# A 39-iteration software pipeline on one core: router products in four column groups, a new order on every engine, and another start

## The chip, the cores and the metric

The kernel runs on one core of a Trainium2 chip. The metric is the device time of one launch in microseconds (us), lower is better. The core has a matrix engine (PE, with its weight loads shown as PEld), a vector engine (DVE), an activation engine (ACT), GpSimd (POOL), and SyncE (SP), which here only issues DMAs. Each engine works through its own list of instructions in order and waits on semaphores for the others.

## The reference

The input x is 8 x 1024 x 256 in float32. Four layers follow one another, each added to a running sum:

```
x = x + gated_linear_attention_and_mlp(layernorm(x))
x = x + mixture_of_experts(layernorm(x))
x = x + tanh_recurrence(layernorm(x))
x = x + mixture_of_experts(layernorm(x))
```

The first layer has its own LayerNorm, a gate `log_sigmoid(h W1 W2 + b) / 16`, a state per head that decays by that gate, a gated output product (`Wo`), and a GELU MLP (`W1`, `W2`). A mixture multiplies every token by all 8 experts (256 x 256), takes router logits (256 to 8), a softmax and the two best experts, and adds the two products with their weights. The recurrence is `h = tanh(x_t B + h A^T)` with 16 states over 1024 steps, then two products.

## The kernel before

**Rounds and stages.** Time is cut into 32 rounds of 32 tokens for all 8 batches, so a round is 256 tokens in two tiles of 128. A round passes through stages, one per iteration; `body(it)` on each engine works on up to eight rounds at once, and `live(it, s)` says whether stage s has one. Iterations 0 to 7 (the fill) are written out, 8 to 31 are a hardware loop, 32 to 38 (the drain) are written out again. The order on each engine is written by hand in its `body`; semaphores count up over the whole launch.

**What stands between what.** The recurrence is the thread on which the rest is strung: `step(k)` on PE (one small product), two tanh on ACT (`state_of(k)`) and one DVE instruction (`split_state(k)`), 32 times a round; each engine has other work between two of them. That work is on PE: `moe` (six products of 512 columns; G1_0 to G1_7 for the first mixture, G2_0 to G2_7 for the second), attention (`scores`, `read_state`, `state_update`, `attend` in 32-wide forms), transposes (T1, T2 of the two mixtures' inputs, Y0, Y1, TR, OG, KT), and the dense products (Z gate, QK, VG, WO, F1, F2).

**The router before.** `logits` takes the transposed tokens `yT` as weights, in two parts (a leading part and its rest), and multiplies by `rws`, the router's two-part weights: for each of 2 tiles and 2 chunks one product of 16 columns and one of 8. The result stands by token, ready for `top_two` on DVE. `yT` comes from T1 by an ACT copy (`lead1`, the leading part) and a DVE subtraction (`rest`, its line is L931).

**Banks.** PSUM has eight banks; `BANK_ORDER` lists who uses each in turn, and `readers` derives from it what PE waits for before it overwrites one.

**ACT's tables.** The gate needs Exp, then Ln, then (after DVE) Exp again; `preload_act_table_set` loads a table ahead of each.

Of the kernel before, what the change touches and what calls it, by code (L numbers as in the profile page):

```python
# [6 lines left out]
F32 = mybir.dt.float32  # L7
# [6 lines left out]
P = 128  # L14
B, T, D = 8, 1024, 256
TS = 32
# [22 lines left out]
PAIRS = E // 2  # L39
GROUPS = TILES * PAIRS  # L40
# [15 lines left out]
    0: [("G2_6", 7, ("acc2", 2 * VECTOR_GROUPS, 10)), ("SD", 2, 'dstate'), ("T2", 6, 'yT2'), ("L2", 6, 'sub2'),  # L56
            ("G1_6", 4, ("acc1", 2 * VECTOR_GROUPS, 10)), ("VG1", 1, 'sg1')],
    1: [("SD", 2, 'dstate'), ("L1", 4, 'sub1'), ("G1_3", 4, ("acc1", 2 * VECTOR_GROUPS, 6)),
            ("G2_1", 6, ("acc2", 2 * VECTOR_GROUPS, 2)), ("G2_5", 6, ("acc2", 2 * VECTOR_GROUPS, 8))],
    2: [("SD", 2, 'dstate'), ("T1", 4, 'yT1'), ("G1_1", 4, ("acc1", 2 * VECTOR_GROUPS, 2)), ("Z", 1, 'zb'),  # L60
            ("G2_0", 6, ("scaled2", 2 * TILES, 2)), ("G2_4", 6, ("scaled2", 2 * TILES, 4)), ("VG0", 1, 'sg0')],
    3: [("SD", 2, 'dstate'), ("Y0", 1, 'hTs'), ("G1_2", 4, ("acc1", 2 * VECTOR_GROUPS, 4)), ("F1A", 3, ("gT", FB, 2)),
            ("G2_3", 6, ("acc2", 2 * VECTOR_GROUPS, 6)), ("TR", 4, 'yrT')],
    4: [("RO", 6, 'mv_m2'), ("O", 2, 'onorm')],
    5: [("RB", 5, ("rnn_h", TS, TS))],
    6: [("KT", 2, 'ktok'), ("F2", 4, 'mv_m1'), ("G2_7", 7, ("acc2", 2 * VECTOR_GROUPS, 12)), ("Y1", 3, 'h2Ts'),
            ("G1_5", 4, ("acc1", 2 * VECTOR_GROUPS, 8)), ("F1B", 3, ("gT", FB, 4)), ("QK", 1, 'qt')],
    7: [("OG", 3, 'oTs'), ("WO", 3, 'mv_f'), ("G1_0", 4, ("scaled1", 2 * TILES, 2)), ("G1_4", 4, ("scaled1", 2 * TILES, 4)),
            ("G1_7", 4, ("acc1", 2 * VECTOR_GROUPS, 12)), ("G2_2", 6, ("acc2", 2 * VECTOR_GROUPS, 4))],
# [25 lines left out]
def build(nc, x, wts, out):  # L95
    ctx = ExitStack()
    with ctx:
# [35 lines left out]
        rw, rws = sb("rw", [P, KC, E]), sb("rws", [P, KC, 2, E], F32R)  # L133
# [91 lines left out]
        def raw(base, n):  # L225
# [4 lines left out]
        early_scalar = [(cst[:], wts["consts"]), (lnw[:], wts["ln_w"]), (lnb[:], wts["ln_b"]), (b2g[:], wts["gk_b2"]),  # L230
                        (raw(W_K, KC * P), wts["Wk"])]
# [67 lines left out]

        block = ctx.enter_context(nc.Block())  # L300


        @block.sync
        def _(sp):
            def load_x(dst, n, name):
# [13 lines left out]
            for dst, src in late_sync[:6]:  # L319
                sp.dma_start(dst, src).then_inc(sem("late"), 16)  # L320
# [1318 lines left out]
```

## Time and profile before

| | before |
|---|---|
| median of 3 runs | 1713.2 us (1711.98 to 1713.89) |
| profiled execution: time | 1721.39 us |
| its span, first to last instruction | 1719.6 us |
| mean granted PE clock, share of full speed | 0.969 |
| busy: PE, PEld, DVE, ACT, POOL | 1606.5, 1369.4, 1241.1, 1033.7, 819.2 us |
| matmul instructions | 16712 |

The profiled execution is 8.2 us longer than the median. A busy time is the sum of one engine's instructions; PE's are pipelined with ends that are modelled, so differences between starts say more than lengths.

### The profile page before, as it was taken

What the parts mean: (1) busy time and instruction counts of PE and PEld (TensorE: products, weight loads), DVE (VectorE), ACT (ScalarE), POOL (GpSimd) and SP (SyncE); (2) the same over time, 40 slices, a digit from 0 to 9 for tenths busy, and PEclk for the clock granted to TensorE, in tenths of its full rate; (3) what the DMA queues carried; (4) which work ended last, traced back from release to release, by engine and by line L of the source; (5) the groups of instructions that cost most, each with busy time, mean ns of one, the idle gap of its engine ahead of it and who ended that gap; (6) DMA issues with size and microseconds to landing.
All of it is one profiled execution on the core that took longest, in us unless ns stands there. A gap on an engine that the chain in (4) does not pass through costs nothing.

```text
span 1719.6 us, 51323 instructions
## 1 busy us (share of the span) xinstructions
PE 1606.5 (93%) x16712; PEld 1369.4 (80%) x16712; DVE 1241.1 (72%) x4557; ACT 1033.7 (60%) x3791; POOL 819.2 (48%) x1293
## 2 busy tenths in 40 slices
PE   3688999999999999999999999999999999998866
PEld 2577788888888888888888888888888888887755
DVE  4566677777778777777787777777877777766544
ACT  4655566666666666666666666666666666654431
POOL 2654445545555455455554554555545545542211
PEclk8798899999999999999999999999999999999978
DMA  4311111111111111111111111111111111110000
GB/s 130 101 57 44 51 56 45 40 39 49 49 55 55 55 44 38 39 49 49 55 55 55 44 38 39 49 49 55 55 55 44 39 39 50 45 51 7 7 7 12
DMA packets 116881, 81.48 MB, mean 47 GB/s; under 512 B 41648, under 2 KB 107856, under 8 KB 116688
## 3 DMA queue, kind: packets, MB, share of 16 engines
q1 hardware_dynamic: 115168, 78.92, 15.3%
q10 hardware_dynamic: 1648, 1.72, 0.3%
q8 instruction: 37, 0.61, 0.1%
q14 instruction: 28, 0.23, 0.0%
HBM read 47.06 MB, written 33.55 MB: 47 GB/s over the span
## 4 chain that ended last, share of the span: by engine, by line
PE 88%; DVE 4%; issue 2%; ACT 2%; POOL 2%; DMA 1%; SPq 0%; POOLq 0%; DVEq 0%; ACTq 0%
PE ps L1229 68%; PE ps L1235 4%; PE ps L1246 3%; PE ps L1302 2%; PE ps L1260 2%; PE ps L1272 2%; PE ps L1262 2%; PE ps L1338 2%; PE ps L1292 1%; DVE yT L931 1%; PE ps L1283 1%; ACT yT L658 1%; DVE hs L836 1%; POOL orstd L467 1%; ACT h_lead L557 0%
## 5 line engine op out<-in xcount | busy, mean ns | idle before, releaser
L1229 PE MATMUL ps<-we,yT 128*128 128x512 f32 x3072 | 832.6, 415 | 0.0
L1229 PEld LDWEIGHTS ps<-we,yT 128*128 128x128 f32 x3072 | 551.0, 192 | 103.9
L557 ACT ACTIVATE h_lead<-ps 48x8 fp32r<-48x8 f32 x1024 | 174.5, 170 | 548.3 <-PE ps L1246 543.2
L836 DVE SCALAR_TENSOR_TENSOR hs<-ps,cst,h_lead 48x8 fp32r<-48x8 f32 x1024 | 224.8, 219 | 262.5 <-ACT ps L558 260.8
L1246 PEld LDWEIGHTS ps<-hs,aT 128*128 128x128 f32 x1024 | 196.0, 191 | 99.0 <-DVE hs L836 77.7
L1246 PE MATMUL ps<-hs,aT 128*128 128x8 f32 x1024 | 210.2, 205 | 35.3 <-DVE hs L836 35.0
L868 DVE SCALAR_TENSOR_TENSOR stage<-ps,coef,stage 128x256 f32<-128x256 f32 x384 | 183.5, 478 | 43.4 <-POOL stage L424 24.5
L868 DVE SCALAR_TENSOR_TENSOR acc<-ps,coef,acc 128x256 f32<-128x256 f32 x384 | 180.9, 477 | 38.9 <-POOL acc L424 26.3
L422 POOL TENSOR_TENSOR part<-part 128x256 f32<-128x256 f32 x64 | 47.2, 737 | 298.3 <-ACT part L575 298.3
L467 POOL TENSOR_TENSOR orstd<-omean,mhalf 128x32 f32<-128x32 f32 x32 | 174.1, 5440 | 2.7
L558 ACT ACTIVATE ps<-ps 48x8 f32<-48x8 f32 x1024 | 163.6, 160 | 0.0
L1229 PE MATMUL ps<-wa,gTs 128*128 128x256 f32 x768 | 106.5, 288 | 0.6 <-ACT ktok L793 0.6
L1229 PE MATMUL ps<-wa,hTs 128*128 128x512 f32 x384 | 105.8, 413 | 0.0
L1229 PE MATMUL ps<-h2Ts,wa 128*128 128x256 f32 x768 | 104.1, 285 | 0.0
L1229 PEld LDWEIGHTS ps<-h2Ts,wa 128*128 128x128 f32 x768 | 97.9, 190 | 4.2
L422 POOL TENSOR_TENSOR stage<-stage 128x256 f32<-128x256 f32 x64 | 47.1, 736 | 113.5 <-ACT stage L575 112.8
L1229 PEld LDWEIGHTS ps<-wa,gTs 128*128 128x128 f32 x768 | 94.9, 190 | 1.2 <-issue 1.2
L1229 PEld LDWEIGHTS ps<-wa,hTs 128*128 128x128 f32 x384 | 69.2, 193 | 14.1
L1260 PE MATMUL ps<-rws,yT 128*128 128x16 f32 x256 | 62.0, 265 | 18.8 <-DVE yT L931 18.8
L392 POOL TENSOR_SCALAR r<-mv 128x2 f32<-128x2 f32 x64 | 12.3, 193 | 135.0 <-DVE mv L855 135.0
L1260 PEld LDWEIGHTS ps<-rws,yT 128*128 128x128 f32 x256 | 51.0, 199 | 23.4 <-DVE yT L931 22.0
L566 ACT ACTIVATE ps<-ps,lnb,lnw 128x256 f32<-128x256 f32 x128 | 62.3, 521 | 9.2 <-PE ps L1235 9.1
(179 smaller groups left out, 3235.5 us busy)
## 6 DMA issues: line engine op xcount, KB each, us to landing
arow<-att SPq DMA_DIRECT2D x32, 512.0 KB, 2.8
atx<-arow SPq DMA_DIRECT2D x128, 128.0 KB, 2.9
xin<-in_x SPq DMA_DIRECT2D x64, 128.0 KB
xag<-in_x SPq DMA_DIRECT2D x64, 128.0 KB
vrow<-vtok SPq DMA_DIRECT2D x32, 256.0 KB, 2.1
vx<-vrow SPq DMA_DIRECT2D x128, 64.0 KB, 2.0
out<-stage SPq DMA_DIRECT2D x64, 128.0 KB
stage<-in_experts SPq DMA_DIRECT2D x1, 2048.0 KB, 10.2
```

The lines of the kernel that those rows point to most:

```text
L422: g.tensor_tensor(m.part[:, i, 0, :], m.part[:, i, 0, :], m.part[:, i, 1, :], ALU.add).then_inc(sem(f"part{m.s}"), 1)
L467: g.tensor_tensor(orstd[:], omean[:], mhalf[:], ALU.pow).then_inc(sem("orstd"), 1)
L557: a.activation(h_lead[:], ps[0:NB, BANK["RB"], k * B:(k + 1) * B], ACT.Tanh)
L558: a.activation(h_whole, ps[0:NB, BANK["RB"], k * B:(k + 1) * B], ACT.Tanh).then_inc(sem("rnn_tanh"), 1)
L566: a.activation(ps[:, bank, c * TOK:(c + 1) * TOK], ps[:, bank, c * TOK:(c + 1) * TOK], ACT.Identity, bias=lnb[:, c:c + 1], scale=lnw[:, c: ...
L836: v.scalar_tensor_tensor(hs[0:NB, :, k], h_whole, keeps_rest, h_lead[:].bitcast(F32), ALU.mult, ALU.subtract).then_inc(sem("rnn_h"), 1)
L868: v.scalar_tensor_tensor(m.acc[:, i, :], ps[:, bank, half * D:(half + 1) * D], m.coef[:, i, e:e + 1], m.acc[:, i, :], ALU.mult, ALU.add).t ...
L1229: ins = t.matmul(dst, left(lp, c), right(rp, c), start=(n == 1), stop=(n == 3 * chunks))
L1235: ins = t.transpose(ps[:, dst_bank, c * TOK + i * P:c * TOK + (i + 1) * P], src[:, i, c * P:(c + 1) * P], ident)
L1246: return t.matmul(ps[0:NP, BANK["RB"], k * B:(k + 1) * B], aT[:], hs[:, :, (k - 1) % TS], start=False, stop=True, skip_group_check=True)
L1260: t.matmul(ps[:, bank, o:o + 2 * E], m.yT[:, 0, c, rows], rws[:, c].rearrange("p s e -> p (s e)"), start=(c == 0), stop=False, skip_group_ ...
L1262: ins = t.matmul(ps[:, bank, o:o + E], m.yT[:, 1, c, rows], rws[:, c, 0, :], start=False, stop=(c == KC - 1), skip_group_check=True)
```

## The change

**Router.** `rw` becomes 128 x 2 x 32 (8 columns of weights, 24 of zero) and is the weight operand. `yT` moves, 256 columns at once, as plain fp32. There are four products (two parts by two chunks), each into its own 32 partitions of the bank, that is its own column group of PE's array. ACT copies that bank's half to SBUF (`lT1`, `lT2`), PE turns it by two transposes (`logits_by_token`), and `top_two` adds up four pieces instead of two. `rws` and the two instructions that split it are gone.

**Order.** All five engines' bodies are written in a new order, and the loop's cut stands elsewhere (PE's begins with G2_0), which by itself moves nothing within an engine.

**Fill.** The first table holds Ln and Exp. In iterations 2 and 3 that table serves the whole gate and `exp_and_others` follows it; in 3 and 4 it is loaded ahead of the Y0 affine step. Round 0's x comes as eight DMAs of one batch each, four issued by SP and four by ACT ahead of ACT's other issues, x for the residual (`xag`) by eight more on SP, and the late weights that ACT issued are issued by SP.

```diff
-        rw, rws = sb("rw", [P, KC, E]), sb("rws", [P, KC, 2, E], F32R)
+        rw = sb("rw", [P, KC, ROUTED])
...
+        def load_first(eng, dst, i, name):
+            for q in range(BQ):
+                eng.dma_start(dst[q * TS:(q + 1) * TS, i, :], x[i * BQ + q, 0:TS, :]).then_inc(sem(name), 16)
...
-            load_x(xin, 0, "x_loaded")
+            load_first(sp, xin, 0, "x_loaded")
             for dst, src in early_sync:
                 sp.dma_start(dst, src).then_inc(sem("early"), 16)
-            load_x(xag, 0, "x_again")
+            for i in range(TILES):
+                load_first(sp, xag, i, "x_again")
             sp.wait_ge(sem("pads_zero"), 1)
             sp.wait_ge(sem("early"), EARLY)
-            for dst, src in late_sync[:6]:
+            for dst, src in late_scalar + late_sync[:6]:
...
+            load_first(act, xin, 1, "x_loaded")
...
-            a.preload_act_table_set("exp_and_others")
+            a.preload_act_table_set("natural_log_exp_and_others")
...
-            for dst, src in late_scalar:
-                act.dma_start(dst, src).then_inc(sem("late"), 16)
...
+                    if filling(it) and it > 2:
+                        a.preload_act_table_set("natural_log_exp_and_others")
                     act.wait_ge(sem("Y0"), c2)
                     affine(BANK["Y0"], "hT", 0)
+                if live(it, 6):
+                    state_of(8, c6)
+                if live(it, 2):
                     affine(BANK["Y0"], "hT", 1)
+                if live(it, 6):
+                    state_of(9, c6)
+                if live(it, 5):
+                    act.wait_ge(sem("LT1"), c5)
+                    a.activation(m1.y[:, 0, :], ps[:, BANK["L1"], 0:TOK], ACT.Copy).then_inc(sem("lT1"), 1)
...
-                halves = ps[:, bank, 0:TILES * 2 * E].rearrange("p (i s e) -> p i e s", s=2, e=E)
-                v.tensor_reduce(m.lg, halves, AX.X, ALU.add).then_inc(sem(f"lg{m.s}"), 1)
+                pieces = ps[:, bank, TOK:2 * TOK].rearrange("p (i s w) -> p i s w", i=TILES, w=ROUTED)[:, :, :, 0:E]
+                v.tensor_reduce(m.lg, pieces.rearrange("p i s e -> p i e s"), AX.X, ALU.add).then_inc(sem(f"lg{m.s}"), 1)
...
+                for part in range(2):
+                    for c in range(KC):
+                        g = part * KC + c
+                        ins = t.matmul(ps[ROUTED * g:ROUTED * (g + 1), bank, 0:TOK], rw[:, c, :], m.yT[:, part, c, :].bitcast(F32),
+                                       start=True, stop=True, skip_group_check=True)
+                return ins
+
+            def logits_by_token(m, bank):
+
                 for i in range(TILES):
-                    for c in range(KC):
-                        rows, o = slice(i * P, (i + 1) * P), i * 2 * E
-                        t.matmul(ps[:, bank, o:o + 2 * E], m.yT[:, 0, c, rows], rws[:, c].rearrange("p s e -> p (s e)"),
-                                 start=(c == 0), stop=False, skip_group_check=True)
-                        ins = t.matmul(ps[:, bank, o:o + E], m.yT[:, 1, c, rows], rws[:, c, 0, :],
-                                       start=False, stop=(c == KC - 1), skip_group_check=True)
+                    ins = t.transpose(ps[:, bank, TOK + i * P:TOK + (i + 1) * P], m.y[:, 0, i * P:(i + 1) * P], ident)
                 return ins
```

**PE, steps 5 to 9 of the recurrence.** Before, in a full written-out iteration (`ps<-hs,aT` is a recurrence step, here steps 5, 6, 7 and 8; `wa,oTs` is the second half of WO; `we,yT` is G2_7; `ym`, `y`, `stage` are T1, Y0 and T2; `rws` the logits):

```order
L1246 MATMUL ps<-hs,aT 128x8
L1292 MATMUL ps<-vtok,ktok 32x64 x16
L1229 MATMUL ps<-wa,oTs 128x256 x6
L1246 MATMUL ps<-hs,aT 128x8
L1229 MATMUL ps<-we,yT 128x512 x6
L1246 MATMUL ps<-hs,aT 128x8
L1235 MATMUL ps<-cst,ym 128x128 x4
L1235 MATMUL ps<-cst,y 128x128 x4
L1235 MATMUL ps<-cst,stage 128x128 x4
L1246 MATMUL ps<-hs,aT 128x8
L1260 MATMUL ps<-rws,yT 128x16
L1262 MATMUL ps<-rws,yT 128x8
```

The same place in the changed kernel, from the state update ahead of step 5 to step 10's predecessor (`yT,rw` are the four router products, `ym 128x128 x2` their transposes):

```order
L1321 MATMUL ps<-vtok,ktok 32x64 x32
L1271 MATMUL ps<-hs,aT 128x8
L1254 MATMUL ps<-we,yT 128x512 x6
L1271 MATMUL ps<-hs,aT 128x8
L1254 MATMUL ps<-wa,oTs 128x256 x6
L1271 MATMUL ps<-hs,aT 128x8
L1260 MATMUL ps<-cst,ym 128x128 x4
L1271 MATMUL ps<-hs,aT 128x8
L1260 MATMUL ps<-cst,y 128x128 x4
L1260 MATMUL ps<-cst,stage 128x128 x4
L1285 MATMUL ps<-yT,rw 32x256 x4
```

G2_7 and the half of WO have changed places, step 8 stands directly behind T1, and the state update is whole ahead of step 5.

**DVE, the same stretch.** Before (`hs<-ps` is a `split_state`, first and last here 5 and 8; `att` are the score masks, `yT<-ps,yT` is the subtraction that the first router waits for):

```order
L925 TENSOR_TENSOR att<-ps,cst 128x2x8x32 x2
L1062 TENSOR_TENSOR dstate<-ps,cst 128x512
L836 SCALAR_TENSOR_TENSOR hs<-ps,cst,h_lead 48x8
L1074 TENSOR_TENSOR xmid<-ps,xhat 128x512
L846 BN_STATS st_f<-xmid 128x6 x2
L836 SCALAR_TENSOR_TENSOR hs<-ps,cst,h_lead 48x8
L931 TENSOR_TENSOR yT<-ps,yT 128x512
```

Changed:

```order
L947 TENSOR_TENSOR att<-ps,cst 128x2x8x32
L858 SCALAR_TENSOR_TENSOR hs<-ps,cst,h_lead 48x8
L947 TENSOR_TENSOR att<-ps,cst 128x2x8x32
L1075 TENSOR_TENSOR dstate<-ps,cst 128x512
L858 SCALAR_TENSOR_TENSOR hs<-ps,cst,h_lead 48x8
L881 TENSOR_SCALAR y<-xin,mv_a,ra 128x256
L1091 TENSOR_TENSOR xmid<-ps,xhat 128x512
L858 SCALAR_TENSOR_TENSOR hs<-ps,cst,h_lead 48x8
L868 BN_STATS st_f<-xmid 128x6 x2
L953 TENSOR_TENSOR yT<-ps,yT 128x512
```

A split stands between the masks, one half of y0 has come in, and `xmid` stands ahead of a split.

**ACT, the first round's gate.** Before (`ge` are the Exp and Ln of the gate, `eq`, `ek`, `emid` the decays, `qx` the masked queries):

```order
L715 ACTIVATE ge<-ge 128x256
L719 ACT_TABLE_LOAD
L721 ACTIVATE ge<-ge 128x256
L723 ACT_TABLE_LOAD
L749 ACT_TABLE_LOAD
L607 ACTIVATE eq<-grel 128x256
L608 ACTIVATE ek<-grel 128x256
L609 ACTIVATE emid<-gcum 128x8
L597 ACTIVATE qx<-qt,cst 128x256
```

Changed:

```order
L752 ACTIVATE ge<-ge 128x256
L759 ACTIVATE ge<-ge 128x256
L616 ACTIVATE eq<-grel 128x256
L617 ACTIVATE ek<-grel 128x256
L618 ACTIVATE emid<-gcum 128x8
L794 ACT_TABLE_LOAD
L606 ACTIVATE qx<-qt,cst 128x256 x2
```

Three loads have become one, and it stands between the decays and the masked queries.

## Rows read from the trace of the kernel before

**Rows 1.** The page: busy time, and the PE clock in 40 slices

```profile
PE 1606.5 (93%) x16712; PEld 1369.4 (80%) x16712; DVE 1241.1 (72%) x4557; ACT 1033.7 (60%) x3791; POOL 819.2 (48%) x1293
...
PEclk8798899999999999999999999999999999999978
```

**Rows 2.** Windows: length, busy PE, PEld, DVE, ACT, POOL, clock, DMA

```profile
56.00:88.00 32.00, 20.13 (x339) 17.10 (x339) 20.50 (x37) 21.39 (x39) 17.76 (x22) 0.75 0.25 74
129.00:181.00 52.00, 44.09 (x459) 37.39 (x459) 29.70 (x105) 28.32 (x110) 21.49 (x35) 0.84 0.13 42
...
600.00:649.00 49.00, 48.42 (x523) 41.52 (x522) 37.86 (x143) 31.55 (x119) 25.41 (x40) 1.00 0.16 48
...
1652.00:1719.60 67.60, 43.00 (x158) 33.88 (x157) 25.78 (x105) 14.39 (x77) 8.46 (x16) 0.78 0.04 12
```

**Rows 3.** Timeline of SP: the issue of the next x, once per iteration

```profile
295.26 1.42 SPq L307 DMA_DIRECT2D xin<-in_x  x2
...
344.31 1.45 SPq L307 DMA_DIRECT2D xin<-in_x  x2
```

**Rows 4.** Waits of PE over the span: total us, times, longest

```profile
PE ps L1246 <- DVE hs L836: 35.0, 56, 1.7
PE ps L1260 <- DVE yT L931: 18.8, 33, 1.5
```

**Rows 5.** Timeline of PE in the loop: step 7 to step 9

```profile
634.90 0.27 PE L1246 MATMUL ps<-hs,aT 128*128 128x8 f32 x1
635.13 0.66 PE L1235 MATMUL ps<-cst,ym 128*128 128x128 f32 x4
635.62 0.60 PE L1235 MATMUL ps<-cst,y 128*128 128x128 f32 x4
...
637.20 0.28 PE L1260 MATMUL ps<-rws,yT 128*128 128x16 f32 x1 [0.52 <-DVE yT L931]
...
638.11 0.25 PE L1246 MATMUL ps<-hs,aT 128*128 128x8 f32 x1
```

**Rows 6.** Timeline of PE in the loop: column groups, plain fp32

```profile
598.42 0.65 PE L1302 MATMUL ps<-vx,atx 128*32 128x64 f32 x32
...
624.39 1.07 PE L1338 MATMUL ps<-stage,bin_ 128*128 128x256 f32 x4
```

**Rows 7.** Timeline in the loop: DVE and ACT ahead of the router

```profile
631.38 0.40 DVE L859 TENSOR_SCALAR y<-xin,mv_a,ra 128x256 f32<-128x256 f32 x1
...
632.75 1.29 DVE L925 TENSOR_TENSOR att<-ps,cst 128x512 f32<-128x512 f32 x2
...
634.76 0.67 DVE L1074 TENSOR_TENSOR xmid<-ps,xhat 128x512 f32<-128x512 f32 x1
...
635.47 0.75 DVE L846 BATCH_NORM_STATS2 st_f<-xmid 128x6 f32<-128x256 f32 x2
...
635.82 0.60 ACT L658 ACTIVATE yT<-ps 128x512 fp32r<-128x512 f32 x1
...
636.45 0.69 DVE L931 TENSOR_TENSOR yT<-ps,yT 128x512 fp32r<-128x512 f32 x1
```

**Rows 8.** Timeline of ACT: the first round's gate

```profile
19.81 1.28 ACT L719 ACT_TABLE_LOAD   x1
...
21.54 1.28 ACT L723 ACT_TABLE_LOAD   x1
...
24.12 0.42 ACT L607 ACTIVATE eq<-grel 128x256 f32<-128x256 f32 x1
...
25.51 0.51 ACT L597 ACTIVATE qx<-qt,cst 128x256 f32<-128x256 f32 x1 [0.56 <-DVE qt L968]
```

**Rows 9.** Timeline: the first x, and SP's issue of the second

```profile
7.97 0.75 DVE L846 BATCH_NORM_STATS2 st_a<-xin 128x6 f32<-128x256 f32 x2 [4.98 <-DMA xin<-in_x]
...
14.31 1.21 SPq L307 DMA_DIRECT2D xin<-in_x  x2
```

**Rows 10.** Timeline of PE in the drain: a bare recurrence step

```profile
1654.35 0.27 PE L1246 MATMUL ps<-hs,aT 128*128 128x8 f32 x1 [0.58 <-DVE hs L836]
```

More of the change, by code:

```diff
@@ L616, in body @@
                         split_late()
+                if live(it, 6):
+                    state_of(0, c6)
+                    state_of(1, c6)
                 if live(it, 4):
@@ L702, in body @@
                     scaled(m1, 1, BANK["G1_4"])
-                    scaled_second(m1, 1, BANK["G1_4"])
+                if live(it, 6):
+                    state_of(17, c6)
                 if live(it, 7):
@@ L753, in body @@
                     decays(c2)
+                    if filling(it) and not live(it, 4):
+                        a.preload_act_table_set("exp_and_others")
                 if live(it, 6):
@@ L763, in body @@
                     normed(yr, m1.acc, rr, 0).then_inc(sem("yr"), 1)
+                if live(it, 6):
+                    state_of(27, c6)
                 if live(it, 7):
@@ L772, in body @@
                     mask_queries(0).then_inc(sem("qx"), 1)
+                if live(it, 6):
+                    state_of(28, c6)
                 if live(it, 7):
@@ L998, in body @@
                         scale_out()
+                if live(it, 6):
+                    split_state(30, c6)
+                if live(it, 4):
+                    dve.wait_ge(sem("gT0"), c4)
+                    rest(gTs, gT[:], "gTs")
+                if live(it, 6):
+                    split_state(31, c6)
                 if live(it, 7):
@@ L1032, in body @@
                 if live(it, 5):
-                    split_state(2, c5)
+                    split_state(1, c5)
+                if live(it, 3):
+                    dve.wait_ge(sem("oT_lead"), c3)
+                    rest(oTs, by_chunk("OG"), "oTs")
                 if live(it, 6):
@@ new lines, in body @@
+                if live(it, 6):
+                    step(21, c6)
+                if live(it, 4):
+                    for name, count in readers(it, "F1B"):
+                        pe.wait_ge(sem(name), count)
+                    for f in range(2, 4):
+                        ins = product(ps[:, BANK["F1B"], f % 2 * TOK:(f % 2 + 1) * TOK], lambda p, c: wcols(W_1, p, c, FF, f * P, P),
+                                      lambda p, c: h2Ts[:, p, c, :], KC)
+                    ins.then_inc(sem("F1B"), 1)
@@ L1316, in body @@
+                if live(it, 6):
+                    step(30, c6)
+                if live(it, 5):
+                    pe.wait_ge(sem("yr"), TILES * c5)
+                    for name, count in readers(it, "TR"):
+                        pe.wait_ge(sem(name), count)
+                    transposed(BANK["TR"], yr).then_inc(sem("TR"), 1)
                 if live(it, 2):
@@ L1367, in body @@
                     scores(0)
-                    scores(1)
-                if live(it, 5):
-                    step(2, c5)
                 if live(it, 4):
@@ L1414, in body @@
                     transposed(BANK["T1"], m1.y).then_inc(sem("T1"), 1)
+                if live(it, 5):
+                    step(8, c5)
                 if live(it, 1):
@@ L1506, in body @@
                     moe(m1, 6, BANK["G1_6"]).then_inc(sem("moe1"), 1)
+                if live(it, 5):
+                    step(19, c5)
                 if live(it, 3):
@@ L1514, in body @@
                     ins.then_inc(sem("F1A"), 1)
-                if live(it, 5):
-                    step(19, c5)
                 if live(it, 4):
```

676 lines of the change are left out of this document (329 added, 347 removed).

## The prediction

> **What bounds the kernel now.** I read the page first: PE is busy 1606.5 of 1719.6 us and no other engine passes 1241 [rows 1]. Then the windows, which say where the other 113 us lie [rows 2]: in the loop PE is busy 48.42 of 49.00 us at full clock, in the fill 20.13 of 32 (clock 0.75) and 44.09 of 52 (0.84), and in the last 67.6 us it is 43.00 (0.78). The period of the loop is the distance between two issues of the next x, 344.31 - 295.26 = 49.05 us [rows 3]; 24 iterations run at it, and about five more (6, 7 and 32, 33 with part of 5 and 34) are as full, so a change of a round counts some 29 times. Last the list of PE's waits [rows 4]: 35.0 us for `hs` (the recurrence) and 18.8 us for `yT` ahead of the first router. The first kind lies in fill and drain, since the loop has idle room for only 0.58 us a round. That room is the second kind, once a round, 0.52 us [rows 5]. So three sums are wanted: PE's own work in a round, the wait at the router, and the fill's chain.
>
> **PE's work in a round.** A router block is eight products today, 638.11 - 637.20 = 0.91 us [rows 5], twice a round. The new block has four products of 256 fp32 columns; the trace shows every plain fp32 product as two pieces. At full width four such pieces take 1.07 us to the end of the last, which is some 0.39 long, so 0.68 / 3 = 0.23 us a piece; `attend` has 128x32 pieces of 64 columns, 32 of them in 0.65 us of which the last takes 0.22, so 0.014 us each, where 64 columns at full width would cost 0.23 / 4 = 0.057: four column groups do run side by side [rows 6]. Eight pieces then cost 8 x 0.23 / 4 = 0.46 us. The two transposes cost half of T1's 635.62 - 635.13 = 0.49, so 0.24 [rows 5]. That is 0.70 against 0.91, twice: -0.42 us. I charge 0.1 us back for going into and out of the 32-wide form, since the first block stands alone among full-width work and the second shares it with `attend`: **-0.3 us a round**.
>
> The bounds: were the four groups served one after another, a block would be 8 x 0.23 = 1.84 us plus 0.24, +1.2 us a block. If the copy and the transposes hid nothing, PE would wait for ACT besides: in the first block G1_0 stands between (about 1.5 us) and the ACT copy is half of one that takes 0.60 [rows 7], so that is covered; in the second G1_4 covers it, though ACT has the square of O in front of the copy, and I see under 0.1 us of room there.
>
> The Trainium skill, TensorEngine Tiling (Array Packing), Key Properties, says that changing the tiling mode drains TensorE while distinct tiles work independently. By the first half each router block would pay an entry and an exit. By the small gaps around the 32-wide work of this trace that is 0.1 to 0.2 us each, and the round would gain 0.0 instead of 0.3.
>
> **The wait at the router.** Today T1 starts at 635.13 and the logits at 637.20, 2.07 us: transposes, the ACT copy 0.60, the DVE subtraction 0.69 [rows 5, 7]. PE has Y0, T2 and step 8 to do meanwhile and still waits 0.52. The change leaves that work in place but puts step 8 ahead of Y0, and it swaps G2_7 and the half of WO, so that `xmid`, which needs WO, now comes due between steps 7 and 8 instead of under G2_7. I walk DVE's queue from step 5, with starts as they lie today [rows 7]: the state update is visible 0.25 us behind step 5; mask 0.60 (half of 1.20 between starts), split 0.14, mask 0.60, dstate 0.67, split 0.14, half of y0 0.31, `xmid` 635.47 - 634.76 = 0.71, split 0.14, statistics 0.67, and 0.75 from the start of the subtraction to the logits. The sum is 4.98 us. PE's own work to the same point is G2_7 1.62, WO 0.84, T1 0.1 + 0.49, step 8 0.1, Y0 and T2 0.15 + 0.85, so 4.15. PE therefore waits some 0.8 us there, spread over step 8 (its split stands behind `xmid`) and the logits, against 0.52: **+0.3 us**. The ACT side gives the same: `state_of(8)` now stands behind half of the affine step of Y0, which needs Y0's transposes, which stand behind step 8; step 9 comes some 1.9 us behind step 8, as late as the logits let it. Two other short intervals (step 3 to 4, 4 to 5) are at the bare step's 0.85 us [rows 10], with 0.1 us of waiting at most. Regrouping small pieces saves PE about as many changes of form as it adds, 0.1 us to the good. So a round goes by -0.3 + 0.3 - 0.1 = **-0.1 us**, times 29 = **-3 us**. Ends: no wait left at all gives -0.3 - 0.5 - 0.0 = -0.8; a wait twice what I walk gives +0.4.
>
> **The fill.** In the first gate Ln starts when its load ends, 19.81 + 1.28 = 21.1 [rows 8]. Without it Ln starts at 19.8; DVE's part behind it takes until two further loads would be done, from 21.5 to about 23.5, so the decays start at about 22.2 instead of 24.12: -1.9 us. But the one load left comes between the decays and the masked queries, where ACT has 0.56 us free [rows 8], so 1.28 - 0.56 = 0.7 comes back, and `scores` wait for the queries. Net -1.2, and the same in iteration 3; in iteration 4 one load leaves the path, -1.3. In these iterations that chain, and not PE (20.13 of 32 us [rows 2]), sets the pace: **-3.7 us**. The first x arrives at 7.8 and starts the first statistics at 7.97, after a wait of 4.98 [rows 9]; eight issues on two queues could bring it up to 1.3 us sooner, but ACT's weights are issued some 2.4 us later for it: I take -0.5, ends -1.3 and +1. SP issues six more weights and six more x pieces, about 6 us of issue, so the second x leaves SP at some 17.5 instead of 14.31 [rows 9]; DVE wants it at 25.6, so that is hidden. The last of the late weights (the recurrence's B) would then land about when PE wants them at 25 to 26, which could eat the -1.2 of the first gate: end +1.2. Fill: **-4 us**, from -7 to 0.
>
> **The drain.** Fewer rounds are live, the steps bind at 0.85 us each, and PE runs at half clock part of the time [rows 2, 10]. The last router block is on the bare path: ACT copy and transposes come in, 0.2 us of products go out: **+1 us**.
>
> **Sum.** -3 - 4 + 1 = -6 us, on the profiled execution 1721.39 to 1715.4; it lies 8.2 above the median, so the median goes from 1713.2 to **1707**.
>
> **The rivals.**
> 1. *The new order hides the router's wait.* If `rest` gets its turn as soon as the copy is there, the round loses 0.8 us instead of 0.1: 29 x -0.8 - 3 = -26, **1687**. For it: PE, DVE and ACT all have idle time on average (DVE 37.86 of 49). Against it: the walk above. Chance 0.20.
> 2. *A longer wait on the other side.* `split_state(7)` stands behind `xmid`. Should DVE get to it 0.5 us later than I walk (ACT's normalised tiles late, for instance), step 8, the logits and step 9 all move: +0.4 a round, 29 x 0.4 - 3 = +9, **1722**. It decides from +0.2 us a round. For it: three things of the stretch now hang on one another, where before one wait of 0.52 took up all lateness. Chance 0.25.
> 3. *The column groups don't overlap at 256 columns.* +1.2 us a block, 64 blocks: +77 - 6, **1784**. Against it: `attend` [rows 6]. Chance 0.04.
> 4. *The order is a draw and the fill gives nothing*, because SP's longer list makes the late weights late: **1712**, within 0.2%. Chance 0.11.
>
> My own forecast has 0.40. The chip tells 0.2% of this kernel, 3.4 us, from nothing. Faster by more: 0.20 of rival 1 and most of mine, 0.57. Within: 0.11 and the upper edge of mine, 0.16. Slower: 0.27. The range reaches to rivals 1 and 2 and leaves out rival 3: **1685 to 1724**; mine alone is 1699 to 1713. The clock may move either way in the fill, where 0.84 of 52 us at half or full speed is worth several us [rows 2]; the range holds that.
>
> **What would show it.** A period of about 48.95 us between x issues; a router block of about 0.5 us in four 32-wide products; waits for `hs` inside the loop at step 8, which today has none, and a wait for `yT` of 0.3 to 0.6. Decays of the first gate near 22 us. A period of 48.3 proves rival 1, 49.4 rival 2, over 51 rival 3. An x issue period as forecast with a median off by more than 8 us would mean that fill or drain moved in a way that I don't see.

## The result and the profile after

The changed kernel takes 1707.93 us in the median of 14 runs (1700.11 to 1712.80); the kernel before, measured beside it, 1717.37 (1711.98 to 1724.27, 14 runs). The ratio is 0.9942, interval 0.9926 to 0.9958: faster by 0.6%, some 10 us. The profiled execution took 1704.93 us, 16.5 less than that of before. It lies 3.0 us below the median of its kernel, and that of before 4.0 us above its own, so the two traces differ by 7 us more than the medians do.

The profile's page, with the span, the busy times and the PE clock, answers to [rows 1]:

```profile
span 1703.1 us, 51651 instructions
...
PE 1596.0 (94%) x16840; PEld 1328.1 (78%) x16840; DVE 1277.2 (75%) x4556; ACT 1050.9 (62%) x3851; POOL 823.7 (48%) x1294
...
PEclk7798999999999999999999999999999999999978
```

Windows of the changed kernel (length, busy PE, PEld, DVE, ACT, POOL, clock, DMA): the second full interval of the fill, one round of the loop, the drain. They answer to [rows 2]:

```profile
122.80:171.20 48.40, 41.86 (x462) 34.33 (x463) 30.39 (x106) 29.02 (x113) 21.15 (x32) 0.89 0.14 45
616.10:665.10 49.00, 48.49 (x528) 40.72 (x527) 39.30 (x143) 32.29 (x122) 25.55 (x40) 1.00 0.16 48
1623.00:1703.00 80.00, 52.49 (x212) 39.02 (x210) 33.64 (x131) 20.76 (x106) 12.71 (x24) 0.81 0.03 10
```

In a round PE is as busy as before: 48.49 of 49.00 us. SP's issues of the next x, as in [rows 3], twice in one usual round and twice around a long one:

```profile
432.87 1.44 SPq L314 DMA_DIRECT2D xin<-in_x  x2
483.21 1.43 SPq L314 DMA_DIRECT2D xin<-in_x  x2
...
679.51 1.43 SPq L314 DMA_DIRECT2D xin<-in_x  x2
728.49 1.44 SPq L314 DMA_DIRECT2D xin<-in_x  x2
```

A usual round is 48.98 us here. The periods given from here on are sums of 32 parts: for each interval between two recurrence steps the median over 20 rounds, so that a delay in single rounds doesn't enter. By this the period is 49.01 us against 49.13 before. But many rounds are longer, two take 50.3 between the starts of step 0, and the mean from iteration 8 to 31 is 49.20, no less than before. PE's waits, as in [rows 4]:

```profile
PE ps L1271 <- DVE hs L858: 38.9, 82, 1.3
...
PE ps L1254 <- issue: 6.6, 23, 0.3
...
PE ps L1285 <- DVE yT L953: 3.9, 5, 1.5
```

The wait for `yT` has left this list in the loop (5 times instead of 33); the next rows show that some of it is still there. In its place stands a wait on no other engine: "issue", 23 times, as often as the loop of 24 iterations branches back. PE at step 5, then from step 7 to step 10, as in [rows 5], and DVE's subtraction that the first router needs, as in [rows 7]:

```profile
623.96 0.27 PE L1271 MATMUL ps<-hs,aT 128*128 128x8 f32 x1
...
626.38 0.23 PE L1271 MATMUL ps<-hs,aT 128*128 128x8 f32 x1
626.58 0.66 PE L1260 MATMUL ps<-cst,ym 128*128 128x128 f32 x4
627.46 0.27 PE L1271 MATMUL ps<-hs,aT 128*128 128x8 f32 x1 [0.23 <-DVE hs L858]
627.66 0.63 PE L1260 MATMUL ps<-cst,y 128*128 128x128 f32 x4
628.12 0.60 PE L1260 MATMUL ps<-cst,stage 128*128 128x128 f32 x4
628.71 0.64 PE L1285 MATMUL ps<-yT,rw 128*32 128x256 f32 x8
629.32 0.27 PE L1271 MATMUL ps<-hs,aT 128*128 128x8 f32 x1
629.46 1.63 PE L1254 MATMUL ps<-we,yT 128*128 128x512 f32 x6
630.93 0.38 PE L1292 MATMUL ps<-cst,ym 128*128 128x128 f32 x2
...
627.99 0.67 DVE L953 TENSOR_TENSOR yT<-ps,yT 128x512 fp32r<-128x512 f32 x1
```

The router's eight pieces take 629.32 - 628.71 = 0.61 us instead of 0.91. The logits seem to start at once behind T2, but they start 0.05 us behind the end of the subtraction (627.99 + 0.67 = 628.66), as they did before (637.14 and 637.20), and so in the median of 20 rounds of either kernel. T2 takes 0.59 us to the next start where Y0 takes 0.46, so about 0.13 us of the wait for `yT` is left. The list doesn't have it, because T2's modelled end covers it.

Where the new stall sits, at the seam between two runs of the loop's body:

```profile
597.80 0.21 PE L1271 MATMUL ps<-hs,aT 128*128 128x8 f32 x1
598.32 1.65 PE L1254 MATMUL ps<-we,yT 128*128 128x512 f32 x6 [0.31 <-issue]
```

Step 20 starts at 597.80 and G2_0 0.52 us behind it, where G1_0 follows step 9 by 0.14 us. The change moved TensorE's loop cut: the body used to begin behind TR, ahead of `kt`'s transposes; now it begins between step 20 and G2_0.

The start: the first statistics, and ACT's first gate, as in [rows 8, 9]:

```profile
4.91 0.75 DVE L868 BATCH_NORM_STATS2 st_a<-xin 128x6 f32<-128x256 f32 x2 [1.91 <-DMA xin<-in_x]
...
19.26 0.42 ACT L616 ACTIVATE eq<-grel 128x256 f32<-128x256 f32 x1 [2.07 <-DVE grel L961]
```

So the first statistics come 3.06 us earlier and the first decays 4.86 us earlier. The three intervals between `bin_` products from iteration 33 on, in the drain, took 47.97, 46.99 and 45.46 us before and 46.13, 44.30 and 44.13 now.

### The profile page after: what moved, and what is told of

It is laid out like the page before. It is cut to its first block, busy times and chain, and to the rows that moved or that the text cites. A ratio compares the mean times of both kernels' runs of the same rounds, so it can differ in the third digit from the quotient of the medians.

```text
span 1703.1 us, 51651 instructions
## 1 busy us (share of the span) xinstructions
PE 1596.0 (94%) x16840; PEld 1328.1 (78%) x16840; DVE 1277.2 (75%) x4556; ACT 1050.9 (62%) x3851; POOL 823.7 (48%) x1294
## 4 chain that ended last, share of the span: by engine, by line
PE 80%; DVE 6%; issue 4%; DMA 4%; ACT 2%; SPq 2%; POOL 1%; ACTq 0%; DVEq 0%; POOLq 0%
PE ps L1254 61%; PE ps L1260 4%; PE ps L1271 3%; DMA xag<-in_x 2%; PE ps L1285 2%; PE ps L1301 2%; PE ps L1440 2%; PE ps L1321 2%; PE ps L1331 1%; PE ps L1312 1%; DVE hs L858 1%; DVE att L947 1%; DMA arow<-att 1%; DVE dstate L1075 1%; PE ps L1292 1%
## 5 line engine op out<-in xcount | busy, mean ns | idle before, releaser
L1254 PEld LDWEIGHTS ps<-we,yT 128*128 128x128 f32 x3072 | 545.0, 190 | 110.2 <-issue 9.7
L1271 PE MATMUL ps<-hs,aT 128*128 128x8 f32 x1024 | 214.3, 209 | 40.3 <-DVE hs L858 38.9
L1254 PE MATMUL ps<-h2Ts,wa 128*128 128x256 f32 x768 | 108.0, 291 | 3.5 <-DVE h2Ts L953 3.5
L512 POOL TENSOR_SCALAR omean<-oss 128x32 f32<-128x32 f32 x32 | 8.9, 277 | 181.1 <-DVE oss L1172 181.1
L575 ACT ACTIVATE ps<-ps,lnb,lnw 128x256 f32<-128x256 f32 x128 | 67.2, 529 | 30.5 <-PE ps L1260 30.5
L401 POOL TENSOR_SCALAR ra<-mv_a 128x2 f32<-128x2 f32 x32 | 6.1, 192 | 146.4 <-DVE mv_a L877 146.4
L606 ACT ACTIVATE qx<-qt,cst 128x256 f32<-128x256 f32 x128 | 64.4, 505 | 0.2 <-DVE qt L977 0.2
```

The source lines that it names most:

```text
L575: a.activation(ps[:, bank, c * TOK:(c + 1) * TOK], ps[:, bank, c * TOK:(c + 1) * TOK], ACT.Identity, bias=lnb[:, c:c + 1], scale=lnw[:, c: ...
L606: return a.activation(qx[:, h, :, :], bt(qt[:]), ACT.Identity, scale=headmask[:, h:h + 1])
L1254: ins = t.matmul(dst, left(lp, c), right(rp, c), start=(n == 1), stop=(n == 3 * chunks))
L1271: return t.matmul(ps[0:NP, BANK["RB"], k * B:(k + 1) * B], aT[:], hs[:, :, (k - 1) % TS], start=False, stop=True, skip_group_check=True)
```

## Experiments

Times are medians of 5 to 12 runs; ratios are to the kernel before on the same chip, which had medians of 1716.9 to 1720.3 us. Where a kernel's profile is quoted, it is of one execution.

**The start alone, in the old kernel** (x by batch element from two queues, Wk first, late weights from SP).

```
-            load_x(xin, 0, "x_loaded")
+            load_first(sp, xin, 0, "x_loaded")
...
             a = nc.scalar
+            load_first(act, xin, 1, "x_loaded")
...
-            for dst, src in late_sync[:6]:
+            for dst, src in late_scalar + late_sync[:6]:
```

> The kernel before with the change's start alone: the first x in one DMA for each batch element, half of them issued by ACT, the second x by batch too, Wk first among ACT's early loads, and the late weights issued by SP. Theory A (the fill is one chain from the first statistics on): the first statistics begin near 4.9 us instead of 7.97 us, as in the changed kernel's trace, and the end comes 3 us earlier (ratio 0.998), which makes the prediction's 0.5 us for this part a term that was mis-sized by a factor of six. Theory B (the later stages of the fill wait for other things): the first statistics move by the same 3 us, but the product with bin_ of iteration 8 comes less than 1 us earlier, and the time is that of before.

Measured: 1715.59 us, ratio 0.9988 (0.9971 to 1.0005). The first statistics start at 4.38 us, 3.6 earlier, and `attend` of iteration 2 3.7 us earlier (38.62 against 42.28), so theory A has the mechanism. `bin_` of iteration 8, by which the expectation told the theories apart, starts at 272.10 us against 280.29; but that start isn't stable to better than 3.7 us between kernels with the same fill (below). The end is 2 us earlier with an uncertainty of 3.

**The tables alone, in the old kernel.**

```
-            a.preload_act_table_set("exp_and_others")
+            a.preload_act_table_set("natural_log_exp_and_others")
...
-                    a.preload_act_table_set("natural_log_exp_and_others")
+                    if not filling(it):
+                        a.preload_act_table_set("natural_log_exp_and_others")
```

> The kernel before with the change's table loads in the fill alone (one set with logarithm and exponential ahead of the first gate, none between; loaded ahead of the first affine in iterations 3 and 4). Theory A (the prediction's): 1.2 us in the first gate and as much in the second, 1.3 us in iteration 4, together -3.7 us (ratio 0.998). Theory B (from the changed kernel's trace, whose attend of iteration 3 leads by no more than that of iteration 2): the first gate gives 1.3 to 1.9 us, the second nothing, together -1.5 us. Theory C: nothing at all.

Measured: 1718.46 us, ratio 0.9998 (0.9981 to 1.0014). `attend` of iteration 2 is 1.6 us earlier (40.69), of iteration 5 0.4 us (152.93 against 153.32). The first gate gives what was expected of it, the later iterations add nothing that shows, and the time is that of before: theories B and C, not the prediction's 3.7 us.

**The router alone, in the old order.**

```
-                    logits(m1, BANK["L1"]).then_inc(sem("L1"), 1)
+                    logits(m1, BANK["L1"]).then_inc(sem("LT1"), 1)
...
                     moe(m1, 0, BANK["G1_0"]).then_inc(sem("moe1"), 1)
+                    pe.wait_ge(sem("lT1"), c4)
+                    logits_by_token(m1, BANK["L1"]).then_inc(sem("L1"), 1)
```

> The kernel before with the change's router alone, in the old order: the four products in column groups, ACT's copy of their result, two transposes, and the sum over four pieces. The DVE step that reads the logits stands one recurrence step later, behind the transposes, all else where it was. Theory A (PE's work sets the loop's period): 0.44 us less work a round (1.82 in two blocks before, 1.38 in two blocks and two pairs of transposes in the changed kernel's trace), the period falls from 49.13 to 48.7, the time by 12 to 14 us (ratio 0.992 to 0.993). Theory B (something beside PE's work takes what it frees, waits for hs above all): period 49.0 to 49.2 and the time within 3 us of before, with more wait for hs. Theory C (the recurrence steps behind the two new hand-offs come late): period above 49.3, slower by more than 5 us.

Measured: 1786.45 us, ratio 1.0400 (1.0377 to 1.0422), period 51.62: theory C, and by far more than it said. PE's waits of this kernel:

```profile
PE ps L1251 <- DVE hs L841: 61.6, 104, 1.4
PE ps L1240 <- DVE y L864: 52.8, 33, 6.8
```

The old order has the transposes of `y1` ahead of step 11, and DVE writes `y1` behind the logits' sum. That sum now comes later, so PE waits some 1.3 us a round for `y1`, and step 10 to 11 takes 3.59 us instead of 1.87. Step 15 to 16 takes 1.59 instead of 0.83 as well, and the waits for `hs` rise from 35.0 to 61.6 us; there DVE now has the second logits' sum ahead of a state. In the changed kernel Y1 stands behind step 13.

**The changed kernel with the loop cut back at its old place.** The order of TensorE's instructions is the same; only the place of the branch differs.

```
             def body(it):
-                if live(it, 7):
...
-                    moe(m2, 0, BANK["G2_0"]).then_inc(sem("moe2"), 1)
...
-                    transposed(BANK["TR"], yr).then_inc(sem("TR"), 1)
                 if live(it, 2):
                     pe.wait_ge(sem("kt"), c2)
...
                     step(20, c5)
+                if live(it, 6):
...
+                    moe(m2, 0, BANK["G2_0"]).then_inc(sem("moe2"), 1)
...
+                    transposed(BANK["TR"], yr).then_inc(sem("TR"), 1)
```

> The changed kernel with TensorE's loop cut back where it was: the stretch from G2_0 to TR stands at the end of the body again, with stage numbers one lower, so that the order of all instructions is that of the changed kernel and the branch stands between TR and the transposes of kt instead of between step 20 and G2_0. Theory A (the branch's 0.31 us of 'issue' before G2_0, 23 times and 6.6 us in the changed kernel's waits, is a cost of the place of the cut): the period falls by 0.2 to 0.3 us to about 48.8, and the time is 5 to 7 us below the changed kernel's. Theory B (the branch costs as much at either place, or another wait takes its place): the same period, 49.1, and a time within 2 us of the changed kernel's.

Measured: **1696.91 us, ratio 0.9873 (0.9851 to 0.9895)**, 11 us below the changed kernel, and the intervals don't touch. The period is 48.67 instead of 49.01, and G2_0 follows step 20 by 0.07 us:

```profile
597.00 0.21 PE L1270 MATMUL ps<-hs,aT 128*128 128x8 f32 x1
597.07 1.64 PE L1253 MATMUL ps<-we,yT 128*128 128x512 f32 x6
...
612.17 0.64 PE L1259 MATMUL ps<-cst,stage 128*128 128x128 f32 x4
612.65 0.38 PE L1344 MATMUL ps<-cst,kt 128*128 128x128 f32 x2
```

The second pair is where the branch is now; it leaves no gap: 612.65 - 612.17 = 0.48 us, and the same two groups stand 0.48 us apart in the changed kernel, which has no branch there. Theory A, and somewhat more than it said.

**The cut one product further on, behind G2_0.**

```
             def body(it):
-                if live(it, 7):
...
-                    moe(m2, 0, BANK["G2_0"]).then_inc(sem("moe2"), 1)
                 if live(it, 6):
                     step(21, c6)
...
                     step(20, c5)
+                if live(it, 6):
...
+                    moe(m2, 0, BANK["G2_0"]).then_inc(sem("moe2"), 1)
```

> The changed kernel with TensorE's loop cut moved by one product: G2_0 alone goes to the end of the body (stage 6 there), so the branch stands behind G2_0's six products of 512 columns and ahead of step 21. The order of all instructions is that of the changed kernel. Theory A (the branch costs where TensorE's queue is empty behind it: in the changed kernel it follows step 20, one short product that the sequencer has just waited for, and G2_0 starts 0.52 us after step 20 instead of 0.07 us): the six long products cover it, the period is 48.7 us as with the cut at its old place, and the time some 10 us below the changed kernel's (ratio to before 0.986 to 0.990). Theory B (only the old place, behind TR's transposes with no recurrence step near, is free): period 49.0 to 49.2 and a ratio of 0.993 to 0.996.

Measured: 1699.78 us, ratio 0.9892 (0.9863 to 0.9921), period 48.62. Theory A: behind six long products the branch costs nothing either:

```profile
598.00 0.20 PE L1272 MATMUL ps<-hs,aT 128*128 128x8 f32 x1
598.06 1.64 PE L1255 MATMUL ps<-we,yT 128*128 128x512 f32 x6
599.54 0.23 PE L1272 MATMUL ps<-hs,aT 128*128 128x8 f32 x1
```

**The old kernel with the cut at the new place.** The converse of the two above.

```
             def body(it):
+                if live(it, 7):
...
+                    moe(m2, 0, BANK["G2_0"]).then_inc(sem("moe2"), 1)
...
                     step(20, c5)
-                if live(it, 6):
...
-                    moe(m2, 0, BANK["G2_0"]).then_inc(sem("moe2"), 1)
```

> The kernel before, its order of instructions unchanged, with TensorE's loop cut put where the change has it: between step 20 and G2_0. Theory A (the cut's place alone costs 0.4 to 0.45 us a round): G2_0 starts 0.5 us behind step 20, the period rises from 49.13 to 49.55, the time by some 10 us (ratio 1.005 to 1.007). Theory B (the cost depends on the new order around it, where TensorE has no slack, and the old order's waits for yT and hs absorb it): period 49.1 to 49.3 and a ratio of 0.999 to 1.003.

Measured: 1730.17 us, ratio 1.0082 (1.0054 to 1.0110), period 49.57, of which step 20 to 21 has 2.07 instead of 1.58 us:

```profile
605.33 0.26 PE L1247 MATMUL ps<-hs,aT 128*128 128x8 f32 x1
605.91 1.64 PE L1230 MATMUL ps<-we,yT 128*128 128x512 f32 x6 [0.33 <-issue]
```

Theory A: the place alone costs 0.43 us a round here and 0.34 in the new order. 23 rounds at 0.43 make 10 us; the medians say 14 (9 to 19).

**The old router in the new order**, with the cut at its old place: eight products into the tokens' own layout, no copy, no transposes.

```
-                       ins = t.matmul(ps[ROUTED * g:ROUTED * (g + 1), bank, 0:TOK], rw[:, c, :], m.yT[:, part, c, :].bitcast(F32),
-                                      start=True, stop=True, skip_group_check=True)
+                        t.matmul(ps[:, bank, o:o + 2 * E], m.yT[:, 0, c, rows], rws[:, c].rearrange("p s e -> p (s e)"),
+                                 start=(c == 0), stop=False, skip_group_check=True)
```

> The changed kernel with the loop cut at its old place (period 48.68) and the old router in the new order: two blocks of eight products into the tokens' own layout, no copy on ACT, no transposes, the old sum over halves. Theory A (TensorE's work alone sets the period in the new order, and the router's part of it is 1.82 us against 1.38): the period is 49.1 us, 0.44 above, and the time 13 us above that kernel's, ratio to before near 0.994. Theory B (the gain comes from the order, which hides the wait for yT, and not from the router's work; without its copies ACT and DVE are freer): period 48.7 or less, ratio 0.987 or less.

Measured: 1711.73 us, ratio 0.9968 (0.9952 to 0.9985), against 0.9873 with the new router. Period 48.98, between the two theories. By intervals between steps in the median of 20 rounds, the new router saves 0.30 (8 to 9) and 0.46 us (14 to 15) and costs 0.16 (9 to 10) and 0.17 us (16 to 17) for the transposes: 0.43 us less work. But step 10 to 11 takes 1.67 instead of 1.50 us, because DVE sums the logits ahead of that step's state. So 0.3 a round is left, and the new order alone is worth 49.13 - 48.98 = 0.15. The medians give the router in this order more than that, 0.9968 - 0.9873 or some 16 us, good to about 5; the loop has 8 of them and the drain's three intervals some 4.

These kernels also show the drain. Windows from step 8 to step 12 in rounds 27, 28 and 29, counted from 0, the last two in the drain; first the kernel before, then the changed one, then the old router in the new order (rounds 28 and 29):

```profile
1471.60:1478.50 6.90, 6.38 (x38) 5.37 (x37) 5.95 (x32) 3.96 (x16) 2.21 (x4) 1.00 0.38 99
1520.50:1528.80 8.30, 7.76 (x34) 6.45 (x35) 5.53 (x31) 2.51 (x13) 2.27 (x5) 0.79 0.41 103
1568.00:1576.30 8.30, 7.77 (x34) 6.47 (x35) 5.54 (x31) 2.48 (x13) 1.42 (x4) 0.79 0.11 34
```

```profile
1461.80:1468.70 6.90, 6.88 (x41) 4.96 (x41) 5.63 (x30) 3.55 (x15) 2.56 (x5) 1.00 0.44 117
1510.40:1517.10 6.70, 6.21 (x37) 4.72 (x38) 5.49 (x32) 2.26 (x12) 2.35 (x5) 1.00 0.46 122
1555.50:1562.20 6.70, 6.21 (x37) 4.72 (x38) 5.49 (x32) 2.26 (x12) 2.09 (x3) 1.00 0.09 24
```

```profile
1505.10:1513.40 8.30, 7.84 (x35) 6.37 (x36) 5.41 (x32) 1.93 (x11) 2.27 (x4) 0.79 0.45 113
1553.90:1560.70 6.80, 6.34 (x36) 5.29 (x36) 5.37 (x32) 1.96 (x11) 2.04 (x3) 1.00 0.09 25
```

With the old router the clock falls to its lower level behind the block of 8- and 16-column products, in round 28 of all five kernels that have it (0.79 over the window) and in round 29 of the four in the old order. In none of the eight kernels with the new router does it fall in these windows, and the old order with the new router is one of these: its two windows take 8.3 us too, at full clock, since PE waits there for `y1`. In the new order round 28's window is 6.65 us with the new router and 8.32 with the old. The next round, 30, gives part of this back. The same window in the kernel before and in the changed kernel with the cut moved back:

```profile
1615.40:1623.60 8.20, 7.23 (x32) 6.00 (x31) 4.76 (x27) 2.76 (x13) 0.10 (x1) 0.79 0.10 32
...
1593.40:1603.30 9.90, 9.47 (x40) 6.89 (x38) 4.27 (x26) 2.59 (x13) 0.00 (x0) 0.61 0.09 28
```

In the eight kernels with the new order, whichever router they have, this window takes 8.6 to 10.2 us at a clock of 0.59 to 0.71, in the changed kernel 8.65.

**The second half of y0 ahead of the late weights' splitting, in iteration 2.**

```
+                    if isinstance(it, int) and it == 2:
+                        normed(y0, xin, mv_a[:, :, 0], ra[:, 6, :], 1).then_inc(sem("y0"), 1)
                         split_late()
```

> The changed kernel with the loop cut at its old place, and in iteration 2 the second half of y0 on DVE ahead of the splitting of the late weights, for which TensorE waited 7.6 us in one piece. Theory A (that wait is on the fill's chain): the transposes of y0 in iteration 3 begin 5 to 7 us earlier, and bin_ of iteration 8 and the end 2 to 6 us earlier than with the cut alone (ratio to before near 0.985). Theory B (the fill's chain goes by the late weights and the first attend of iteration 2, which stand behind it): the same time within 2 us of the kernel with the cut alone (0.9873).

Measured: 1698.32 us, ratio 0.9897 (0.9872 to 0.9923). The longest wait for `y` falls from 7.6 to 3.9 us, but one of 5.4 us for the scores that `attend` reads appears, and the `attend` of iteration 3 comes 1.5 us later (67.42 against 65.88). Theory B by the median. `bin_` of iteration 8 does start 4.5 us earlier in this trace, at 268.61 against 273.10, as theory A had it, but the time shows nothing of it.

**Half of xhat behind step 19 instead of 15.** One of the changed kernel's two longest rounds, at DVE:

```profile
442.94 0.41 DVE L881 TENSOR_SCALAR xhat<-xag,nrm 128x256 f32<-128x256 f32 x1 [1.46 <-DMA xag<-in_x]
...
444.26 0.21 DVE L858 SCALAR_TENSOR_TENSOR hs<-ps,cst,h_lead 48x8 fp32r<-48x8 f32 x1
```

SP began to issue that x at 434.52, 8.4 us earlier; the state of step 16 stands behind it on DVE. The other one, at iteration 8, has 0.3 us of this and 0.8 of something else, ahead of step 5:

```profile
278.59 0.17 PE L1271 MATMUL ps<-hs,aT 128*128 128x8 f32 x1 [0.83 <-issue]
```

That one waits for nothing that the profile shows. It comes in the three kernels of the new order whose cut stands at G2_0 or one product behind it, and in none of the five with the cut at its old place.

> The changed kernel with the loop cut at its old place, and the first half of xhat on DVE behind recurrence step 19 instead of step 15. In the trace of the changed kernel DVE waits 1.46 us at 441 us for the second copy of x ahead of this half, and the h2Ts half, two sums and the state of step 16 stand behind it, so TensorE's step 17 waits 1.09 us; such delays of the interval from step 16 to 17 were 1.25, 0.32, 0.29, 0.13 and 0.13 us in the changed kernel and 0.84 and 0.62 us with the cut alone. Theory A (the transfer is issued just in time and its landing varies): with the half four steps later no round from iteration 9 on is more than 0.2 us above the usual 48.68, mean of the loop 48.68 instead of 48.78, time 2 us lower (ratio to before 0.984 to 0.987). Theory B (the longer rounds come from elsewhere, and the wait for x is only their sign): still one or two rounds of 49.5 or more.

Measured: 1697.16 us, ratio 0.9885 (0.9867 to 0.9904). No round is long any more, so theory A has the cause of most of them, but every round is 0.2 us longer between steps 20 and 21 (1.74 against 1.54): period 48.91. The half now stands in front of a state that PE wants. Nothing is won, and a third place wasn't tried.

**DVE's queue from step 7 to 12 in another order**, in the kernel of the last experiment (period 48.91).

```
                 if live(it, 5):
                     split_state(7, c5)
                 if live(it, 3):
                     dve.wait_ge(sem("WO"), c3)
...
                 if live(it, 5):
                     split_state(10, c5)
                 if live(it, 4):
                     dve.wait_ge(sem("L1"), c4)
```

> As the kernel with xhat's half moved, and DVE's queue from step 7 to step 12 put in another order, the same instructions: the states of steps 7 and 8 ahead of xmid and its statistics, yT's half ahead of these, the state of step 10 ahead of the logits' sum, the state of step 11 ahead of the denominators. Theory A (what is left of the router's hand-offs is the wait for hs at step 8, 0.23 us in the trace, and 0.10 to 0.16 us at step 11): both go, the period is 48.68 less 0.2 to 0.3, 48.4 us, and the time 6 to 9 us lower than with xhat's half alone (ratio near 0.981). Theory B (the wait moves on: yT's half comes later behind xmid, and the router's products wait for it): the wait for hs at step 8 goes, one for yT of 0.1 to 0.3 us appears, the period is within 0.1 of 48.68.

Measured: 1738.81 us, ratio 1.0121 (1.0099 to 1.0142), period 50.24. Neither theory. Step 7 to 8 does fall, from 1.08 to 0.81 us, but PE has new waits once a round:

```profile
PE ps L1250 <- DVE hTs L952: 24.0, 30, 2.9
PE ps L1250 <- DVE mv_f L876: 19.3, 31, 0.7
```

The first is G1_2, which needs the PSUM bank that `hTs` reads Y0 from, the second G1_0, which needs the bank of WO, released by the statistics of `xmid`. Steps 9 to 10 (with G1_0) and 11 to 12 (with G1_2) take 2.54 and 2.39 us where they took 1.75 and 1.61. The wait for `yT` is in the list again too, 33 times and 9.6 us in all, as theory B had it. My walk had looked at operands, not at banks.

**The changed kernel with the old start and the old tables.**

```
-            load_first(sp, xin, 0, "x_loaded")
+            load_x(xin, 0, "x_loaded")
...
-                    if not filling(it):
-                        a.preload_act_table_set("natural_log_exp_and_others")
+                    a.preload_act_table_set("natural_log_exp_and_others")
```

> The changed kernel, its loop cut included, with the start and the table loads of before: x in two DMAs by SP, late weights in part by ACT, a logarithm's table loaded behind the first exponential in each iteration. Theory A (start and tables together are worth what the traces show at attend of iteration 5, about 6 to 8 us): first statistics near 8 us, bin_ of iteration 8 later by 5 to 9 us, time above the changed kernel's by as much, ratio to before 0.997 to 0.999. Theory B (stretches of half clock, whose place differs from run to run, take back the earlier start): bin_ of iteration 8 within 3 us, ratio 0.994 to 0.996.

Measured: 1708.50 us, ratio 0.9954 (0.9936 to 0.9972), against 0.9942 with the new ones. `attend` of iteration 2 is 3.8 us later (41.60), `bin_` of iteration 8 2.5 us (272.27 against 269.78). Theory B: start and tables together are worth 2.5 to 3 us in the traces, and the medians can't tell it from nothing. Whether stretches of half clock take the rest back isn't shown.

## Why the prediction came out right

The forecast was 1707 us and the measurement 1707.9. That near a hit is luck: the forecast took 6 us from 1713.2, a median of three runs, and 14 runs of that kernel give 1717.4; the gain is 9.4 us (0.6%) where 6 was forecast (0.3 to 0.4%). And the loop hit the usual round by errors that cancel: the router's wait was put too high, and the cut wasn't in the sum at all.

- *PE's work*, forecast -0.42 us a round and -0.3 after a charge for changes of form: the work measured -0.43. Column groups overlap at 256 columns; rival 3 is dead. Behind the logits' sum stands a new wait of 0.17 us ahead of step 11, about what the charge was. Right in size. The Trainium skill, TensorEngine Tiling (Array Packing), Key Properties, says that a change of tiling mode drains TensorE. The trace agrees in part: the first block, with full-width work behind it, takes 0.61 us, and the second, with `attend` behind it, 0.46, so some 0.15 us shows once a round, behind the block; what entering costs isn't separated. The round kept its 0.3.
- *The wait at the router*, forecast +0.3 net of today's 0.52, less 0.1 for regrouping: wrong in sign, and both sides of the walk were off. It had the logits 4.98 us behind step 5 with 4.15 us of PE's own work in between, so 0.8 of waiting. They start 628.71 - 623.96 = 4.75 us behind it, with 0.23 us of waiting at step 8 and some 0.13 for `yT`, so about 4.4 of work and 0.36 of waiting. The new order alone gives -0.15 a round. Rival 1 is half true: with the cut at its old place, new order and router bring 49.13 to 48.67, -0.46 a round.
- *The loop's cut*, a term that the sum doesn't have: +0.34 us a round (48.67 to 49.01; in the old order +0.43). That is the step that failed. I read how instructions moved against one another and not where the branch stands among them, and the text ahead of the prediction says that the cut moves nothing. It costs 8 to 14 us, about as much as the whole change gains.
- *Late x*, also missing: `xhat`'s half moved four steps forward and its transfer did not; rounds are longer by up to 1.25 us, some 3 us in the profiled run, and 0.8 us more come at iteration 8 from a stall that goes with the new cut.
- *The fill*, forecast -4: the first x was mis-sized (-0.5 forecast, -3.1 at the first statistics). The tables give 1.6 us in the first gate and next to nothing over the fill, where -3.7 was forecast. What the whole fill is worth stays open. `bin_` of iteration 8 starts at 280.29 and 269.78 us in the two main traces, but at 276.55 in another kernel with the old fill and at 273.10 in another with the new one: the same fill differs by 3.3 to 3.7 us. The new start in the old order brings it to 272.10, and the old start and tables in the new order to 272.27, so either seems to be enough and they don't add up. The medians give the start 2 us, the tables nothing, and both in the new order 2, none of them clear of noise.
- *The drain*, forecast +1: the three intervals measured -5.9 together. This is a lucky execution: six other kernels with the new router and order take 136.1 to 138.8 us for the three, the changed one 134.6, and before took 140.4, so -1.6 to -4.3. Some 3.3 of the 5.9 are the two half-clock windows behind the old router, which are gone, and round 30 gives part of that back, in its window 0.3 to 1.9 us. The copy and transposes on the bare path are there, but small beside that.

Of the signs that the prediction named, step 8 waits for `hs` as it said, and the period of 49.01 is near its 48.95; the wait for `yT` of 0.3 to 0.6 is not there, but some 0.13, and the first decays came at 19.3 and not at 22. The two traces differ by 10.5 us up to `bin_` of iteration 8, by -0.8 over the next 25 iterations (usual rounds -3, long ones +4), by 5.9 in the drain's three intervals and by 0.9 behind. The medians differ by 9.4, and the runs divide it otherwise: order, start and tables together are worth -5.5 us (0.9968), the router in that order -16 more (to 0.9873), and the cut takes 12 back (to 0.9942), the last two good to about 5 us each.

## What to carry to other kernels

A loop's branch has a place among the instructions, and it is a parameter: put it behind a piece of work long enough to cover it (0.48 us of transposes was enough here), never behind a short instruction alone. Read it from the list of waits, where it stands as "issue" once per round. A wait shorter than the modelled end of the work ahead of it is not in that list: compare starts with the end of what the engine waits for. A new form of an operation and the order around it are one change: the same router cost 4% in the old order. And when an engine's queue is re-ordered by hand, buffers that an instruction releases count as much as results that it delivers.

## What the runs showed of the hardware

- The branch of TensorE's loop cost 0.44 to 0.49 us between steps 20 and 21, and 0.34 to 0.43 in the period, where it followed one short product, 0.31 to 0.33 of it shown as "issue"; it cost nothing behind four transposes or six 512-column products. The Trainium skill, Advanced Engine Details and Errata, Control Flow Timing, gives a branch some 0.05 to 0.11 us. By that, an estimate from the page's figures, 23 rounds would lose 1.2 to 2.5 us; the runs show 8 to 14. What makes up the rest isn't shown by any run.
- Eight pieces of 256 fp32 columns in four column groups take 0.46 us (second block) to 0.61 us (first), where four such pieces at full width take 1.07 [rows 6].
- Behind a block of 8- and 16-column products the granted clock fell from 2.4 to 1.2 GHz in the drain's rounds, and it did not with 256-column products in 32-wide groups in the same place. In the loop it fell behind neither. The one drop that any of these kernels has there, in the one with the cut behind G2_0, is at 283 us, ahead of step 8 and 1 us behind a stall of 1.38 us. The wait for `yT` ahead of the block doesn't do it by itself: the new router in the old order has that wait, 0.5 us in rounds 28 and 29, and keeps the full clock. That the column count does it is argued and not shown, since the two blocks differ in length and in form as well; and the old router in the new order has the drop in one round of the two.
- The clock falls elsewhere in the drain too, with either router: in round 29 of three kernels in the new order, for 3.4 us behind step 5, one of them with the old router.
